# Retention stage of a four-layer kernel: the bias add, one pair's expert outputs, the squares, the row sums and the last gate are moved

## What is computed

```python
q = (x @ wq + bq).reshape(b, s, h, dk).transpose(0, 2, 1, 3)      # k and v alike
dmask = jnp.where(diff >= 0, gamma[:, None, None] ** expn, 0.0)
scores = jnp.einsum('bhnd,bhmd->bhnm', q, k) * dmask
ret = jnp.einsum('bhnm,bhmv->bhnv', scores, v)
mean = ret.mean(axis=(2, 3), keepdims=True)
var = ((ret - mean) ** 2).mean(axis=(2, 3), keepdims=True)
norm = (ret - mean) * jax.lax.rsqrt(var + EPS)
norm = norm * gn_w.reshape(h, dv)[None, :, None, :] + gn_b.reshape(h, dv)[None, :, None, :]
gate = jax.nn.silu(x @ wg + bg)
out = gate * ro @ wo + bo                                         # ro is norm, heads joined
...
x = x + _L0_ffn_ref(_layernorm(x, axis=-1), ...)                  # layer 2
x = x + _L0_attn_b_ref(_layernorm(x, axis=-1), ...)               # retention, layer 3
```

## Time and profile before

| | |
|---|---|
| median of 3 runs | 1624.3 us (1621.7 to 1625.3) |
| profiled execution, its time | 1625.95 us |
| profiled execution, its span | 1624.2 us |
| mean granted clock of PE | 0.902 |
| retention in the span | 679.7 to 1071.4 us |
| of it batch 0, 1, 2, 3 | 93.4, 98.8, 98.6, 53.4 us |
| DVE busy in the whole span | 1115.7 us (69%) |
| PE busy in the whole span | 1322.5 us (81%) |

### The profile page before, as it was taken

One profiled execution on the slowest core, in us unless ns is written; L12 is line 12 of the kernel. 1 busy time (PEld: TensorE's weight loads), 2 busy tenths in 40 slices (PEclk: granted clock), 3 DMA queues, 4 the chain that ended last, 5 costly groups with the idle time before them and its releaser, 6 DMA issues. The chain is left out here.

```text
span 1624.2 us, 25154 instructions
## 1 busy us (share of the span) xinstructions
PE 1322.5 (81%) x7400; PEld 882.2 (54%) x7400; DVE 1115.7 (69%) x2766; ACT 680.2 (42%) x1365; POOL 930.7 (57%) x1064
## 2 busy tenths in 40 slices
PE   6688467996999997799887888855999588888664
PEld 2344344664777773456464565642666466666433
DVE  4899887775466563418475573768677488888768
ACT  5999321221566663141404224221121376677520
POOL 3999547776455555264544543017777377777700
PEclk9799768998899997999988889967999799999978
DMA  9900073334777764224335142044232666664178
GB/s 362 388 1 0 5 298 104 107 108 144 238 248 248 252 224 152 63 79 170 138 112 190 41 158 107 2 174 177 103 113 98 201 201 194 208 195 155 29 282 275
DMA packets 116745, 257.61 MB, mean 159 GB/s; under 512 B 22759, under 2 KB 44686, under 8 KB 116116
## 3 DMA queue, kind: packets, MB, share of 16 engines
q1 hardware_dynamic: 88436, 188.51, 33.9%
q0 software_dynamic: 27648, 67.70, 12.3%
q10 hardware_dynamic: 544, 0.00, 0.0%
HBM read 124.76 MB, written 139.75 MB: 163 GB/s over the span
## 5 line engine op out<-in xcount | busy, mean ns | idle before, releaser
L853 POOL DMA_INDIRECT slots_x<-arena,slot x256 | 271.7, 1061 | 104.6 <-issue 74.2
L1185 POOL DMA_INDIRECT pairs_y<-arena x192 | 189.4, 987 | 79.0 <-issue 44.9
L1109 PE MATMUL moe_narrow<-arena 128*128 128x128 f32 x1536 | 209.3, 280 | 30.5 <-DVE arena L1250 29.9
L1109 PEld LDWEIGHTS moe_narrow<-arena 128*128 128x128 f32 x1536 | 188.7, 193 | 42.4 <-issue 42.1
L698 PE MATMUL moe_wide<-arena 128*128 128x512 f32 x384 | 186.7, 633 | 17.9 <-DVE arena L966 17.9
L1250 DVE TENSOR_TENSOR arena<-arena,moe_narrow 64x128 f32<-64x128 f32 x384 | 111.6, 291 | 107.1 <-ACT arena L1152 101.3
L457 POOL DMA_INDIRECT arena<-slots_y,slot x128 | 125.9, 984 | 93.2 <-DMA arena<-slots_y,slot 49.2
L1146 ACT ACTIVATE arena<-moe_narrow 128x512 f32<-128x512 f32 x192 | 114.7, 597 | 108.9 <-PE moe_narrow L1109 55.3
L1098 PE MATMUL moe_narrow<-ident,arena 128*128 128x128 f32 x768 | 128.3, 291 | 21.2 <-DMA arena<-slots_x 21.2
L485 DVE SCALAR_TENSOR_TENSOR residual<-arena,gate,residual 128x256 f32<-128x256 f32 (+1 forms) x256 | 113.0, 514 | 39.4 <-DMA arena<-pairs_y 19.0
L1258 DVE COPY arena<-moe_wide 128x512 f32<-128x512 f32 x192 | 132.8, 692 | 8.8 <-DMA pairs_y<-arena 2.7
(11 more groups left out here) (253 smaller groups left out, 2423.8 us busy)
## 6 DMA issues: line engine op xcount, KB each, us to landing
slots_x<-arena SPq DMA_DIRECT2D x48, 528.0 KB, 4.9
arena<-slots_x SPq DMA_DIRECT2D x96, 264.0 KB, 3.0
slots_x<-arena SPq DMA_DIRECT2D x48, 512.0 KB, 15.2
arena<-slots_x SPq DMA_DIRECT2D x96, 256.0 KB, 3.1
slots_y<-arena SPq DMA_DIRECT2D x96, 256.0 KB, 2.3
arena<-w_gu SPq DMA_DIRECT2D x2, 8192.0 KB
arena<-pairs_y SPq DMA_DIRECT2D x32, 512.0 KB, 4.6
residual<-x SPq DMA_DIRECT2D x8, 512.0 KB, 8.7
```

The lines of the kernel that those rows point to most:

```text
L853: pool.indirect_dma_start(out=x_slots, in_=xn[:, t, :], in_offset=None, out_offset=bass.IndirectOffsetOnAxis(ap=slot[:, t, i:i + 1], axis=0))\
L1109: last = pe.matmul(h_ps[n % 2][:, j * P:(j + 1) * P], weights[:, n % 3, j, h, :], xt[:, n % XTRING, (j * KH + h) * P:(j * KH + h + 1) * P] ...
L1185: pool.indirect_dma_start(out=slots.y_of, in_=ytile[:, n % YRING, j, :], in_offset=None, bounds_check=slots.pairs - 1, oob_is_err=False, o ...
```

## The change

Five edits, all in retention:

1. `add_output_bias(b + 1)` stands on POOL behind the scaling of batch b+1's first half, instead of at the start of batch b+1. `decay_q(b + 1, 0)` now stands behind the second `layernorm_power`.
2. The choices of pair 0 of batch b+2 are added on DVE between `gate(b)` and `keep_values(b + 1, 1)`. In the chunks stand only pair 1's four parts, one in each of chunks 1 to 4. For batch 1 pair 0 is added in the setup. Batch 2 has no such pair, so its body stands apart from the loop on DVE.
3. ACT does `copy_xt(b + 1, 1)` and the reading of m = 0 to 2 ahead of `squares(b)`, and PE has the second group sum behind m = 4 instead of m = 1.
4. `keep_output` is two ACT instructions with `accum_out`, one for each half of the channels, and DVE sums 2x8 numbers for each partition instead of 2x1024.
5. In batch 3 the norm is two numbers per partition, a scale and a shift; ACT applies them by halves of 512 tokens, DVE multiplies with the gates by halves, and PE's output waits for each half.

```diff
+    row_parts = arena.take(CH, TB)
+    group_shift = arena.take(CH)
...
-            def output(b):
+            def output(b, last_one=False):
...
-                    if i == 0:
+                    if i == 0 and not last_one:
                         pe.wait_ge(sem("gated"), CH * (b + 1))
+                    if i % (BLK // 2) == 0 and last_one:
+                        pe.wait_ge(sem("gated"), CH * (b + 1 + i // (BLK // 2)))
...
                 transpose_x(b + 1, 1)
-                project(b + 1, 1, range(2))
+                project(b + 1, 1, range(5))
                 group_sum(b, 1)
-                project(b + 1, 1, range(2, PJ_USES))
+                project(b + 1, 1, range(5, PJ_USES))
                 output(b)
...
             def keep_output(b, j):
                 act.wait_ge(sem("rt_full"), RT_TURN * b + j + 1)
-                act.activation(ret[:, :, j * P:(j + 1) * P], rts[j % 2][:, 0:D].rearrange("p (c n) -> p c n", c=CH), ACT.Copy)\
-                    .then_inc(sem("rt_read"), 1)
+                for c in range(CH):
+                    last = act.activation(ret[:, c, j * P:(j + 1) * P], rts[j % 2][:, c * P:(c + 1) * P], ACT.Identity,
+                                          accum_out=row_parts[:, c, j:j + 1])
+                last.then_inc(sem("rt_read"), 1)
...
                 normalise(b + 1, 1)
+                copy_xt(b + 1, 1)
+                add_bias(b + 1, 1, range(3))
                 squares(b)
-                copy_xt(b + 1, 1)
-                add_bias(b + 1, 1, range(PJ_T))
+                add_bias(b + 1, 1, range(3, PJ_T))
             chunks(B - 1, last_one=True)
             squares(B - 1)
+            act.wait_ge(sem("group_shift"), 1)
+            for h in range(H):
+                for c in range(CH):
+                    half = ret[:, c, h * N:(h + 1) * N]
+                    act.activation(half, half, ACT.Identity, bias=group_shift[:, c:c + 1], scale=group_scale[:, c:c + 1])\
+                        .then_inc(sem("normed"), 1)
...
             for b in range(B - 1):
-                add_output_bias(b)
-                gather(b + 1, range(4 if b else 2, 6))
+                gather(b + 1, [4, 5])
                 layernorm_power(H * (b + 1))
-                gather(b + 1, range(6, TB))
+                gather(b + 1, [6, 7])
                 decay_k(b + 1, 0)
+                layernorm_power(H * (b + 1) + 1)
                 decay_q(b + 1, 0)
-                layernorm_power(H * (b + 1) + 1)
+                add_output_bias(b + 1)
                 if b + 2 < B:
                     gather(b + 2, [0])
                 group_power(b)
...
-                dve.tensor_reduce(sums[:, 0, :], ret, AX_X, ALU.add).then_inc(sem("row_sums"), 1)
+                dve.tensor_reduce(sums[:, 0, :], row_parts, AX_X, ALU.add).then_inc(sem("row_sums"), 1)
...
+            def gate_last(b):
+
+                steps = Chain(dve, sem("gate_steps"), 1 + CH, b)
+                dve.wait_ge(sem("group_rstd"), b + 1)
+                steps.link(dve.tensor_tensor(group_scale, group_scale, gnw, ALU.mult))
+                steps.link(dve.tensor_tensor(group_shift, minus_mean, group_scale, ALU.mult))
+                steps.link(dve.tensor_tensor(group_shift, group_shift, gnb, ALU.add))
+                dve.sem_inc(sem("group_shift"), 1)
+                for h in range(H):
+                    for c in range(CH):
+                        half = ret[:, c, h * N:(h + 1) * N]
+                        dve.wait_ge(sem("normed"), CH * h + c + 1)
+                        dve.tensor_tensor(half, half, gates[:, c, T * b + h * N:T * b + (h + 1) * N], ALU.mult)\
+                            .then_inc(sem("gated"), 1)
...
-                parts = [(0, 1), (2, 3), (4, 5), (6,), (7,)] + [()] * (TB - 5)
+                parts = [(), (4,), (5,), (6,), (7,)] + [()] * (TB - 5)
...
                 gate(b)
+                if more:
+                    add_choices(b + 2, 0)
                 keep_values(b + 1, 1)
                 output(b)
```

More of the change, by code:

```diff
@@ L1783, in _ @@
             group_sum(B - 1, 1)
-            output(B - 1)
+            output(B - 1, last_one=True)
         @block.scalar
@@ L1929, in _ @@
             layernorm_power(1)
-            for t in range(2):
-                choices.gather(pool, TB + t, apart=True)
-            pool.wait_ge(sem("decay"), 16 * 4 * CH)
-            for h in range(H):
-                decay_k(0, h)
-                decay_q(0, h)
-            pool.wait_ge(sem("blocks"), 3)
-            pool.wait_ge(sem("w_o"), 16 * LOADS)
             def gather(b, tiles):
@@ L1940, in gather @@
                     choices.gather(pool, TB * b + t, apart=True)
+            gather(1, [0, 1])
+            pool.wait_ge(sem("decay"), 16 * 4 * CH)
+            decay_k(0, 0)
+            decay_q(0, 0)
+            gather(1, [2])
+            decay_k(0, 1)
+            decay_q(0, 1)
+            pool.wait_ge(sem("blocks"), 3)
+            pool.wait_ge(sem("w_o"), 16 * LOADS)
+            add_output_bias(0)
+            gather(1, [3])
             for b in range(B - 1):
-                add_output_bias(b)
-                gather(b + 1, range(4 if b else 2, 6))
+                gather(b + 1, [4, 5])
                 layernorm_power(H * (b + 1))
-                gather(b + 1, range(6, TB))
+                gather(b + 1, [6, 7])
                 decay_k(b + 1, 0)
+                layernorm_power(H * (b + 1) + 1)
                 decay_q(b + 1, 0)
-                layernorm_power(H * (b + 1) + 1)
+                add_output_bias(b + 1)
                 if b + 2 < B:
@@ L2093, in _ @@
             dve.wait_ge(sem("w_vg"), 16 * LOADS)
-            for h in range(H):
-                keep_values(0, h)
+            keep_values(0, 0)
+            add_choices(1, 0)
+            keep_values(0, 1)
             dve.wait_ge(sem("values_cleared"), 1)
@@ L2109, in _, with batch @@
             dve.wait_ge(sem("w_o"), 16 * LOADS)
-            with dve.Fori(0, B - 1) as b:
+            def batch(b, more=True):
                 chunks(b)
@@ L2119, in _ @@
                 gate(b)
+                if more:
+                    add_choices(b + 2, 0)
                 keep_values(b + 1, 1)
                 output(b)
+            with dve.Fori(0, B - 2) as b:
+                batch(b)
+            batch(B - 2, more=False)
             chunks(B - 1, last_one=True)
@@ L2125, in _ @@
             variance(B - 1)
-            gate(B - 1)
+            gate_last(B - 1)
             output(B - 1)
```

1 line of the change is left out of this document (removed).

## The result

The changed kernel takes **1615.7 us** in the median of four runs (1610.3 to 1616.0), against 1624.5 for the kernel before on the same chip: ratio 0.9941, 95% interval 0.9922 to 0.996. By the medians that is 8.9 us less (6.5 to 12.7 by the interval) where 14 were forecast.

What follows compares the result with a forecast made beforehand. Retention was taken as bound by a chain passing between engines, with DVE setting the pace in the chunks. Batches 0 to 3 at +0.85, -3.5, -8.0 and -3.35 sum to -14.0: 1624.3 to 1610 us, range 1597 to 1620.

Steps and rivals of the forecast that it cites:

- The chain behind the chunks: Second projection, group sum, variance, gate, output: three uses left behind the sum, so PE could begin the output 5.7 us earlier.
- rival B: Second projection still at half clock, group sum 2.7 us later in three batches: +8, 1618 us; chance 0.15.
- Chunks: Chunks 0 to 2 without pair 0 and bias add: 8.15 us saved each in batches 1 and 2, 4.2 in batch 0.
- What takes that place: Batches 0 and 1: behind the gate DVE waits for tile 1, then adds pair 0 beside POOL's scaling; next chunk 4.5 later.
- rival A: No contention in the tail: DVE and POOL work side by side, 12.3 us more saved, 1598 us; chance 0.17.
- I add 1.7 for that: Tails of batches 0 and 1: 1.7 us for PE's lower clock after idling ahead of its third output step.
- 916.05 + 6.4 + 1.7: Third output step's start, usual time to the next chunk, and slow clock: next chunk at 924.1, less 0.2, against 919.4.
- Rival D: No change that can be told: rival B together with one or two us of Rival C per batch, 1621 to 1627; chance 0.10.
- Batch 2: Scaling starts with the gate: gate 4.8 us later, first output step at half speed; end 0.65 later, batch -8.0 in all.
- Bias add at nothing: POOL's bias add, moved behind normalising, ends at 890.6 while DVE waits for the variance until 898.45.
- Last gate and row sums: Batch 3: row sums save 1.8 us and the last gate by halves 1.55, together -3.35.
- Rival C: Tiles 2 and 3 come late among zero writes, chunk 1 waits 7.7 us in three batches: +23, 1633 us; chance 0.08.

Runs made afterwards that it cites:

- e2: Changed kernel with tiles 2 and 3 gathered ahead of POOL's scaling of the second half; ratio to the kernel before 0.9884, retention 327.0 us.
- e4: Changed kernel with POOL waiting for the gate before batch 2's scaling of the second half; ratio to the kernel before 0.9886, retention 325.4 us.
- e6: Changed kernel with the output bias added again at each batch's start; ratio to the kernel before 1.0005, retention 344.3 us.
- e1: Changed kernel with pair 0's choices back in the chunks; ratio to the kernel before 0.9837, retention 320.1 us.
- e7: Changed kernel with the last gate whole on DVE and the output behind all of it; ratio to the kernel before 0.9972, retention 341.7 us.
- v2: Changed kernel with pair 0's parts one behind each output step, tiles 1 to 3 gathered ahead of the scaling; ratio to the kernel before 0.9839.
- v3: v2 with DVE's loop written out and batch 2's scaling on POOL waiting for the gate; ratio to the kernel before 0.9849, retention 326.0 us.
- e8: e1 with squares again ahead of the copies and the second group sum behind m = 1; ratio to the kernel before 0.9857, retention 330.7 us.

## Why the prediction was right, and where it was off

**The chain behind the chunks: right.** First transposes to the second group sum 28.6 us (I had about 29), variance to the gate's end 5.44, output at the gate's end; the second projection at full clock, so rival B did not come.

**Chunks: right in sum** (20.1 us saved, 20.6 forecast), with batch 0 0.8 and batch 1 0.6 short and batch 2 0.9 better. The 0.5 for code outside the loop was too small: a written-out chunk with one part takes 4.64 to 4.71 us instead of 4.91, a plain one 3.85 instead of 3.93, about 1.3 for a batch.

**What takes that place: mechanism right.** Tile 1 was there 4.2 us behind the gate's end; I had 3.9. The seven additions ended 9.7 us behind the gate; I had 9.9. From the rows of layer 1 I had priced the contention at 3.1; e2 shows it directly: 2.6 us. So rival A did not come. The gather of 2.02 us at 899.80, beside a DVE gate instruction with two SBUF inputs, is again against the inference in the Trainium skill (SBUF — State Buffer, section Who interferes with whom) that descriptor generation isn't stalled by such an instruction; the trace here disagrees with it as before.

**The step that failed** is "I add 1.7 for that", and the sum "916.05 + 6.4 + 1.7" built on it. It prices only the third output step at half clock. From the third step's start to the next chunk I had 7.9 us; measured are 9.8 in batch 1 and 11.3 in batch 0 (814.04 to 825.38). The third step itself began 0.5 earlier behind the gate than forecast in both, and took 3.78 us instead of 1.89, 1.9 for my 1.7. The fourth step is slow too: its addition follows the third's by 3.20 and 3.03 us instead of 1.73, 1.5 and 1.3 more. That carries the error of batch 1 (5.9 for 4.65). In batch 0 the pause at the jump back comes on top. From the last addition to the next chunk are 4.39 us against 2.65 in batch 1, 1.7 more. 1.3 + 1.7 = 3.0, the error of batch 0 (7.6 for 4.65). Nothing in my text had that pause. The total looks better than these two batches do: together they missed by 5.6 us, and 1.8 of that came back by luck in batch 2. The median of 1615.7 is 1.7 us beyond the 1606 to 1614 of the sum alone, and inside the whole range. Rival D, which needs B and C, did not come.

**Batch 2: right, 1.8 us better** (half of it the chunks'). The gate was 3.8 later, not 4.8. Without the collision I had the batch's rest 5.6 shorter than before; in e4 it is 5.8 shorter (48.1 against 53.9). The sum for the rest had a slip: its own terms (-0.9, +1.7, +0.15 and -0.2 for the overlap) give about 0.8, not 0.65.

**Bias add at nothing: right, but not what it replaced.** Its 3.8 us in chunk 0 were the price of standing beside L485; with the choices out of that chunk it costs 0.3 to 1.1 (e6). The two parts save the same us once. e1 gives the bias add's share while the choices stay: 4.6 and 5.5 in batches 1 and 2, the second with some 0.9 of code outside the loop in it.

**Last gate and row sums: right, term by term** (-3.3 for -3.35). From the last chunk's first mask the variance comes 2.1 us sooner than before (9.2 for 11.3), by the row sums, where I had 1.8; from the variance to PE's output it is 1.4 less (4.06 for 5.44), as in e7, where I had 1.55; 0.2 goes again in PE's first step. `keep_output` costs 0.2 for each read of the sum, two on the path less the overlap: its wait in the chunks is 2.65 against 2.41 before, 0.25 for my 0.15.

**Rival C did not come** in the changed kernel: chunk 1 waited 0.6 at most. It came in v2 and v3, by the mechanism that it names.

**What stays open:** why the last output step is at half clock in one execution and not in the next; and the pause. It is there in all eight profiles in which the loop is kept and pair 0 stands outside the chunks (3.06 to 3.61 us), and in none of before, e1 and e8, nor in the written-out code. What comes just before the jump doesn't decide: v2 has other instructions there and pauses. In the versions that pause the loop begins ten instructions further on among DVE's records, because batch 1's pair 0 is added in the setup, and a pass of it is one longer (312 against 311). Each of the eight pauses has two packets of the instruction queue in it; at the six other boundaries between batches 0 and 1 there is none. Which of place and length matters was not tried.

## What to carry to other kernels

An idle stretch of an engine is only free if what comes next on the chain isn't queued behind it: pair 0 filled DVE's idle time and cost 24 us in two batches to save 10 in three, and it hid what the reordering of squares was worth (nothing with it, 2.7 a batch without). Ask of each edit what it gives with its neighbours undone, since two can save the same us (choices and bias add) and one can cancel another. Count a difference only from the first place that the edit reaches: of e8's 10.6 us, 8.6 lay ahead of it, where every profile from that chip is longer. One batch can also pay for what the others gain, as batch 2 does for the squares. Where PE is made to wait, allow for half clock in the step behind the first slow one too: here it was slow in some executions and at full speed in others.

## What the runs showed of the hardware that I had not expected

- DVE stood 3.1 to 3.6 us at the loop's jump back, with two packets of an instruction queue, in eight profiles, and not at all in three whose loop begins ten instructions earlier and is one shorter; written out, the same code has no such pause.
- A DVE instruction of two numbers per partition can take 1.23 us instead of 0.16 beside POOL's scaling, and one addition of 0.48 us took 3.32; masks that read PSUM keep their 2.48 us beside a POOL add that stretches their SBUF neighbours from 0.61 to 2.38.
- The wait ahead of a projection didn't tell its clock: eight rows took 3.70 us behind a wait of 1.76, and 5.38 behind one of 0.85.
- The same code had the stretch up to the second transposes 1 to 2 us longer in each batch on another chip (22.4 to 23.6 us against 21.5), while its batch 3 took 50.0 us on both.
- ACT's reading of a sum is an instruction of its own, 0.19 to 0.20 us.
